# Value products in groups of four key tiles, softmax sums turned in 32x32 blocks, and the loads of the projection stage moved

## The reference

```python
q = split_heads(hidden_states @ Wq + bq)          # k and v likewise
scores = jnp.einsum('bhqd,bhkd->bhqk', q, k) / scale
c2p = take_along_axis(q . pos_k, c2p_pos)         # position terms, gathered by bucket
p2c = take_along_axis(k . pos_k, p2c_pos)
scores = scores + (c2p + p2c) / scale
probs = jax.nn.softmax(scores, axis=-1)
ctx = jnp.einsum('bhqk,bhkd->bhqd', probs, v)
out = ctx @ Wo + bo + hidden_states
```

## Time and profile before

| | |
|---|---|
| median of 3 runs | 1821.61 us (1818.94 to 1828.15) |
| profiled execution | 1821.79 us, span 1820.0 us |
| mean granted TensorE clock | 0.953 |
| busy share of the span | PE 89%, DVE 79%, ACT 63%, POOL 57% |
| project ends, attend starts | about 153 us from the start of the span |
| first scores | 185 us |
| last weigh | 1363 us |

### The profile page before, as it was taken

One profiled execution on the slowest core, in us unless ns is written; L12 is line 12 of the kernel. 1 busy time (PEld: TensorE's weight loads), 2 busy tenths in 40 slices (PEclk: granted clock), 3 DMA queues, 4 the chain that ended last, 5 costly groups with the idle time before them and its releaser, 6 DMA issues. The chain is left out here.

```text
span 1820.0 us, 41928 instructions
## 1 busy us (share of the span) xinstructions
PE 1622.9 (89%) x13688; PEld 1139.5 (63%) x13688; DVE 1437.4 (79%) x3848; ACT 1141.6 (63%) x2784; POOL 1040.8 (57%) x1264
## 2 busy tenths in 40 slices
PE   7961799999999999999999999999985866999997
PEld 4530566666666666666666666666643645999996
DVE  4750799999999999999999999999965854555553
ACT  5852577777777777777777777777662741222221
POOL 0001777777777777777777777777813632333332
PEclk9985899999999999999999999999996967999998
DMA  4975879787878787878887878787707725766662
GB/s 141 323 251 176 295 258 301 256 274 246 279 255 286 255 279 253 275 246 281 273 276 244 279 253 275 245 280 253 238 10 170 233 80 166 204 200 194 200 199 65
DMA packets 292451, 421.66 MB, mean 232 GB/s; under 512 B 35383, under 2 KB 233805, under 8 KB 292140
## 3 DMA queue, kind: packets, MB, share of 16 engines
q1 hardware_dynamic: 281000, 388.56, 65.5%
q10 hardware_dynamic: 7491, 21.10, 3.8%
q0 software_dynamic: 3744, 9.31, 1.4%
HBM read 241.39 MB, written 177.79 MB: 230 GB/s over the span
## 5 line engine op out<-in xcount | busy, mean ns | idle before, releaser
L891 ACT ACTIVATE t_probsT<-t_flip 128x512 f32<-128x512 f32 x1024 | 614.4, 625 | 206.5 <-PE t_flip L768 112.8
L821 DVE TENSOR_REDUCE t_most<-t_scores 128x1 f32<-128x640 f32 (+1 forms) x512 | 436.4, 852 | 80.6 <-PE t_scores L745 80.0
L831 DVE CUSTOM_DVE_ANT_0 t_band<-t_scores,t_near,t_most 128x384 f32<-128x384 f32 (+1 forms) x512 | 296.3, 579 | 0.4 <-DVE t_most L821 0.2
L842 DVE TENSOR_SCALAR_CACHE_REDUCE t_band<-t_band,t_top 128x384 f32<-128x384 f32 (+1 forms) x512 | 290.8, 568 | 0.0
L883 ACT COPY t_table<-t_table_ps 128x388 f32<-128x388 f32 x512 | 253.9, 496 | 56.6 <-issue 33.0
L967 POOL TENSOR_TENSOR t_near<-t_near,masks 128x768 f32<-128x768 f32 (+1 forms) x128 | 280.0, 2187 | 0.0
L782 PE MATMUL t_sum_ps<-t_probsT,vals 128*32 128x256 f32 x4096 | 274.3, 385 | 0.3 <-ACT t_probsT L891 0.3
L738 PE MATMUL t_scores<-afters,quests 105*128 105x256 bf16 (+3 forms) x1024 | 242.9, 287 | 21.0 <-DVE t_top L831 20.7
L768 PE MATMUL t_flip<-masks,t_band 128*128 128x128 f32 x1408 | 260.1, 273 | 0.0
L745 PE MATMUL t_scores<-masks,t_near 128*128 128x128 f32 x1408 | 239.8, 273 | 2.5 <-POOLq L970 2.5
L951 POOL TENSOR_TENSOR t_near<-t_near,masks 128x384 f32<-128x384 f32 (+1 forms) x128 | 146.5, 1145 | 111.6 <-DMA t_near<-skew_d 105.7
(11 more groups left out here) (206 smaller groups left out, 2623.2 us busy)
## 6 DMA issues: line engine op xcount, KB each, us to landing
skew_d<-t_table SPq DMA_DIRECT2D x128, 1024.0 KB, 9.2
t_near<-skew_d SPq DMA_DIRECT2D x128, 640.0 KB, 8.1
t_near<-skew_d SPq DMA_DIRECT2D x128, 384.0 KB, 7.1
e_w<-in_L_ffn_W_dram ACTq DMA_DIRECT2D x39, 512.0 KB
e_w<-in_L_ffn_W_dram SPq DMA_DIRECT2D x39, 512.0 KB
split_d<-p_part SPq DMA_DIRECT2D x32, 384.0 KB, 3.4
afters<-split_d SPq DMA_DIRECT2D x128, 96.0 KB
quests<-split_d SPq DMA_DIRECT2D x128, 96.0 KB
```

What stands on the lines that cost most here:

```text
L821: nc.vector.tensor_reduce(most[:, c:c + 1], out[:, wide:S], AX.X, ALU.max).then_inc(far_seen, 1)
L831: nc.vector.tensor_tensor_reduce(band[n % 2][:, t, 0:wide], out[:, 0:wide], near[n % 2][:, 0, t, at:at + wide], 1.0, most[:, c:c + 1], ALU ...
L842: nc.vector.tensor_scalar(band[n % 2][:, t, 0:wide], band[n % 2][:, t, 0:wide], top[n % 2][:, t:t + 1], None, ALU.subtract, ALU.max, accum ...
L891: nc.scalar.activation(probsT[s % 4][:, half * 512:(half + 1) * 512], flip_ps[half][:, :], ACT.Exp, scale=SCALE).then_inc(expd, 1)
```

## The change

Six edits:

- `weigh` runs for four tiles together in every fourth slot (slots 1 and 5), and `probsT` has six buffers in place of four.
- `normalise` turns the sums in 32x32 blocks with a DVE transpose, so that the sums lie in 8 columns; it takes 8 reciprocals per partition, multiplies, and turns back.
- In project the loads of units 0 and 1 move one group earlier, each ahead of that group's writes; the loads of units 2 and 3, of the second far block and of the values leave it. Units 2 and 3 are loaded by SP in attend, the values by ACT.
- In the 20 start-up slots DVE copies every second table, from a second buffer that lies in `scores_ps[1]`.
- ACT lays the constant rows after its first three tables, not before all.
- Waits on tables are split accordingly (`table_kept` by ACT, `early_kept` by DVE).

```diff
-EARLY = 4
+EARLY = 2
@@ project, SP @@
                 if live(s + XB):
                     load(s + XB)
+                if s == 4:
...
+                    hats.load_unit(sp, split_d, 0)
+                if s == 5:
+                    hats.load_unit(sp, split_d, 1)
+                if s == 6:
+                    hats.load_far(sp, far_d, 0)
@@
-                if s == 5:
...
-                    hats.load_unit(sp, split_d, 0)
-                    hats.load_unit(sp, split_d, 1)
-                if s == 6:
-                    hats.load_far(sp, far_d, 0)
-                    hats.load_vals(sp, v_d, 0)
-                    hats.load_unit(sp, split_d, 2)
-                if s == 7:
-                    hats.load_unit(sp, split_d, 3)
-                    hats.load_far(sp, far_d, 2)
@@ attend, SP @@
+            load_unit(EARLY)
             for u in range(-2, N + 3):
...
-                if EARLY <= u + 4 < N:
+                if EARLY < u + 4 < N:
                     load_unit(u + 4)
@@ attend, PE @@
-                if live(back - 1) and back % 2 == 0:
-                    weigh(back - 2)
-                    weigh(back - 1)
+                if live(back - 1) and back % 4 == 0:
+                    for j in range(back - 4, back):
+                        weigh(j)
@@ attend, DVE, normalise @@
-                nc.vector.stream_shuffle(spread[:, :], made[n % 2][:, :], [DH] * 32).then_inc(spread_made, 1)
-                dve.wait_ge(spread_made, n + 1)
-                nc.vector.reciprocal(spread[:, :], spread[:, :]).then_inc(inverse_made, 1)
-                dve.wait_ge(inverse_made, n + 1)
-                nc.vector.tensor_tensor(made[n % 2][:, :], made[n % 2][:, :], spread[:, :], ALU.mult).then_inc(normed, 1)
+                nc.vector.transpose(turned[:, :, :].rearrange("p b f -> p (b f)"), made[n % 2][:, :]).then_inc(sums_turned, 1)
+                dve.wait_ge(sums_turned, n + 1)
+                nc.vector.reciprocal(share[:, :], turned[:, :, DH]).then_inc(share_made, 1)
+                dve.wait_ge(share_made, n + 1)
+                nc.vector.tensor_tensor(turned[:, :, 0:DH], turned[:, :, 0:DH],
+                                        share[:, :].unsqueeze(2).to_broadcast([P, QT, DH]), ALU.mult).then_inc(shared, 1)
+                dve.wait_ge(shared, n + 1)
+                nc.vector.transpose(made[n % 2][:, :], turned[:, :, :].rearrange("p b f -> p (b f)")).then_inc(normed, 1)
@@ attend, DVE, ahead of the first look @@
+            for x in range(1, AHEAD, 2):
+                dve.wait_ge(table_made, x + 1)
...
+                nc.vector.tensor_copy(ends, out[:, :, 0:FEW].rearrange("p a (e v) -> p a e v", e=2))
+                nc.vector.tensor_copy(wide[:, :, LEFT:SPOT - LEFT],
+                                      out[:, :, LEFT - 1:LEFT].to_broadcast([P, 2, SPOT - FEW])).then_inc(early_kept, 1)
@@ attend, ACT @@
-                if s >= 4 and half == 0:
-                    act.wait_ge(summed, s - 3)
+                if s >= 6 and half == 0:
+                    act.wait_ge(summed, s - 5)
@@
-            act.wait_ge(set_up, 4)
-            act.wait_ge(before_set, 3)
-            for dst, src in ((quests[KROWS:FAR, :, :], ones[0:3, :]), (afters[FAR:ROWS, :, :], after_rows[:, :]),
-                             (befores[FAR:ROWS, :, :], before_rows[:, :])):
-                nc.scalar.dma_start(dst, src.unsqueeze(1).to_broadcast([dst.shape[0], BUFS, S])).then_inc(rows_set, 16)
             for s in range(-AHEAD, TS + LAG + 1):
+                if s == 6 - AHEAD:
+                    act.wait_ge(set_up, 4)
+                    act.wait_ge(before_set, 3)
+                    for dst, src in ((quests[KROWS:FAR, :, :], ones[0:3, :]), (afters[FAR:ROWS, :, :], after_rows[:, :]),
+                                     (befores[FAR:ROWS, :, :], before_rows[:, :])):
+                        nc.scalar.dma_start(dst, src.unsqueeze(1).to_broadcast([dst.shape[0], BUFS, S])).then_inc(rows_set, 16)
+                if s == 10 - AHEAD:
+                    hats.load_vals(nc.scalar, v_d, 0)
...
-                if live(s + AHEAD):
+                if live(s + AHEAD) and (s >= 0 or s % 2 == 0):
                     keep_table(s + AHEAD)
```

65 lines of the change are left out of this document (46 added, 19 removed).

## The result

| | before | changed |
|---|---|---|
| median | 1823.16 us (1818.94 to 1828.15, 6 runs) | 1805.18 us (1802.68 to 1811.47, 6 runs) |
| span of the profiled execution | 1820.0 us | 1805.1 us |

The ratio is 0.9904, 95% interval 0.9884 to 0.9924: 18 us or 1.0% faster, where 45 were forecast; 1805 lies above the range of 1748 to 1802. I cut both profiled executions at four points: the start of attend (first memset on POOL), the first and last of the 64 DMA starts of the maxima, and the start of the last copy of sums. The two profiled executions differ by 15 us, and the table adds up to that.

What follows compares the result with a forecast made beforehand. In the steady part PE and ACT handing flip halves to each other set the unit, with DVE's wait covered. Terms: project 15, start-up 7, steady part 22, tail 1, in all 45 off 1821.8: 1777 us, range 1748 to 1802.

Steps and rivals of the forecast that it cites:

- The value products: PE, steady units: two of four groups per unit go, 0.4 us a unit, 25 us over some 62 units.
- the charge for the DMA: Steady units: 0.05 us a unit, 3 us, charged for PE waiting on the DMA of the maxima.
- The DMA of the maxima: Steady units: room before the first flip shrinks to 5.2 us; landing expected at about the edge.
- the second rival: DMA of the maxima lands around 5.6 us, PE waits 0.4 a unit, steady gain nil: 1799 us; chance 0.2.
- The normalise: DVE, each unit: 3.05 us becomes 1.5; counted at nothing in time, since ACT's exponential is late next.
- Project: End of project: last split writes start earlier without loads ahead, attend starts at 138; gain 15 us, bounds 9 and 17.
- The start-up: Start of attend: tables kept earlier by two engines, gain 7 us counted, bounds 3 and 9.
- The tail: End of attend: last normalise shorter by 1.5 us, last burst two tiles longer; gain 1 us.

Runs made afterwards that it cites:

- half_write: Changed kernel with only the first of two tables in each SP table write written from unit 2 on (a probe, output differs): 1784.25 us, ratio 0.9787.
- w_only: Kernel before with only the value products in groups of four and six probability buffers: 1834.87 us, ratio 1.0072.
- lag14: Changed kernel with the flips one slot later and the transpose of the maxima ahead of the burst in slot 2: 1796.81 us, ratio 0.9863 to the kernel before.
- n_only: Kernel before with only the sums turned in blocks in normalise: 1818.47 us, ratio 0.9974.
- wn: Kernel before with the groups of four, the six buffers and the block-turned sums, nothing else: 1811.85 us, ratio 0.9943.
- t_only: Kernel before with only the start-up changed, tables copied on two engines and constant rows laid after three tables: 1815.91 us, ratio 0.9961.
- l_only: Kernel before with only the loads moved out of project: 1816.86 us, ratio 0.9963.
- order_mid: calm_mid with SP's loads of the next units behind the second table write and its read: 1776.82 us, ratio 0.9742 to the kernel before.
- loads_tail: Changed kernel with the loads of units 2 and 3 issued by SP at the end of project: 1802.26 us, ratio 0.9880 to the kernel before.
- calm: loads_tail with each later load of values cut into four pieces in four units: 1793.83 us, ratio 0.9847 to the kernel before.
- calm_mid: calm with the transpose of the maxima between the second and third product of the burst: 1804.85 us, ratio 0.9906 to the kernel before.
- calm_lag14: calm and lag14 together: 1798.43 us, ratio 0.9876 to the kernel before.
- loads_behind: calm with the loads of units 2 and 3 behind group 6's value write in project: 1796.67 us, ratio 0.9858 to the kernel before.

## Why the prediction was wrong, point by point

- **The value products** (22 of the 45, with the charge for the DMA). Of the 22 the 63 units gave 2. The size was right for the compute engines: units of 17.67 exist, and in half_write the 63 units give 24. Two things were wrong. I credited it to the products alone, where w_only is slower than before: DVE, which I had held to be covered, is what PE waits for once the products are in fours, and the cheap normalise is needed for the gain. And I charged 3 us for DMA where about 22 go.
- **The DMA of the maxima.** The step that failed is "I expect the burst to end 0.5 to 0.9 earlier and the DMA to land at about the edge". It landed 5.6 us after its start in the median, as before (5.5), against a room that I had put at 5.2. PE waits 16.9 us for it between 200 and 1300. The second rival had this landing (5.6), this wait and a price near the result (1799); that the price is so near is in part luck, since it has project 4 too small and the start-up 10 too large in gain. By lag14 the wait is about half of the loss of 20. What neither the forecast nor the rival had is the loop in SP's queue, with its turn of 13 us at landings of 8 and 17 at landings of 12. I had read the waits of PE and not those of SP, and held SP's wait for the flips to be what would move the burst forward; it was the slack of the loop, and the forecast spent it. The rule of the Trainium skill ("DMA: Bandwidth & Descriptors", section "Queues, rings and completion order") is that the queues are served in turn, packet by packet. The prediction drew from it that an earlier end of SP's burst would not help, and the traces agree as far as they go: 5.5 and 5.6 us. The rule does not make a small DMA quick here: it takes 2.0 us without SP's table writes beside it, 5.1 with half of them and 5.6 with all.
- **The normalise.** 1.5 us, right. n_only shows that it is worth almost nothing by itself (0.3%), as argued, though what came late next was ACT's table copy (14.3 us) and not its exponential, which PE waits for as long as before (10.0 and 9.6). On top of the products it is worth 24 us: wn has 1129.0 in the 63 units, w_only 1153.3.
- **Project.** Right in mechanism, 4 us more than taken and 2 above its bound. The time from the last issue to the start of attend fell by 3.0 us, for which I had allowed 0.6, and the parts of group 7 were ready 3.3 us earlier, where I let 1.95 come back, a figure for which I showed no row: those of group 6 were already 1.3 us earlier themselves (DVE starts the last of them at 115.37, where it was 116.68).
- **The start-up.** Mis-sized by 10: 7 less was forecast, 2.9 more came. The tables themselves came as worked out. Table 11 is kept 13.3 us after the start of attend (12.8 forecast, 21.8 before):

```profile
147.29 0.28 DVE L904 COPY t_table<-t_scores 128x124 f32<-128x124 f32 x1
```

Two parts of the chain behind them were wrong. Tables made early gave 3.6 (t_only), not 7: the first read of the diagonals starts only 3.8 us earlier, since it stands 7.2 us behind the start of the first table write, where it was 5.5 before. And the two added loads cost 7 (l_only), where my bound let them cost 4. In the changed kernel the load of unit 3 stands between read and write:

```profile
153.65 1.33 SPq L693 DMA_DIRECT2D t_near<-skew_d  x2
155.03 5.67 SPq L178 DMA_DIRECT2D afters<-split_d  x2
160.73 2.22 SPq L178 DMA_DIRECT2D quests<-split_d  x2
163.05 0.60 SPq L683 DMA_DIRECT2D skew_d<-t_table  x1
```

The table write starts 28.8 us after the start of attend, later than the 26.6 of before, and the scores of slot 3 (PE) answer to the earlier trace rows:

```profile
173.45 0.90 PE L773 MATMUL t_scores<-masks,t_near 128*128 128x128 f32 x3 [3.28 <-POOLq L1014]
```

That is 39.2 us after the start, where it was 39.5: the gain of the tables is used up. From there to the first DMA of the maxima it takes another 3 us more than before, because POOL gets the reads of the second unit late and splits the maxima only behind them. PE's first transpose of the maxima, before and in the changed kernel:

```profile
203.80 0.23 PE L790 MATMUL t_table_ps<-t_ident,t_top_part 128*24 128x128 bf16 x1 [0.38 <-POOL t_top_part L987]
```

```profile
187.83 0.28 PE L818 MATMUL t_table_ps<-t_ident,t_top_part 128*24 128x128 bf16 x1 [3.28 <-POOL t_top_part L1031]
```

- **The tail.** I forecast 1 less, it was 3 more. The other kernels with bursts of four have 18.8 to 20.1, where the kernel before has 18.0, so 1 to 2 of the 3 go with the bursts; the cause of the rest is not shown.

What stays open: why the same traffic, once it overlaps, takes half as long again (landing 12 in place of 8). The runs show that it does, and what it followed in these runs, but not the mechanism on the DMA engines. It is also open why the small DMA of the maxima takes 5.6 us beside this traffic and 2.0 without it.

## What to carry to other kernels

Read the waits of the queue that issues the DMAs as closely as those of the compute engines. A queue that waits long for compute has slack; divide it by the number of units, and take off what a faster unit will use of it. Where a load stands between a read and the write that the next read needs, put it behind that write: it costs no byte and gave 28 us here, where the queue's loop had no slack left, and little (4 us, not clear of noise) where it had some. The best kernel of this study that does all of the work is order_mid, 1776.82 us, 2.6% (2.3 to 2.9) below the kernel before.

## What the runs showed that I had not expected

- A program can run at two paces with the same instructions: landings of 8 us and units of 17.8, or 12 us and 18.1. The slower one was seen at the start of the units (loads_tail, calm) and behind one load of 1.15 MB, the values (lag14, wn). loads_tail, calm and wn came out of it again; calm_mid and calm_lag14, whose loop has 0.6 and 1.8 us of slack, did not. What decides is not shown beyond that.
- A 6 KB DMA from an otherwise idle queue landed 5.6 us after its start (median) beside 266 GB/s of other traffic, 5.1 with half of the table writes left out, and 2.0 us when SP wrote no tables.
- SP's issue of the same eight writes takes 4.45 us in the changed kernel, where no loads stand just ahead, and 6.6 to 9.3 where loads do (loads_behind, and the kernel before).
